# An attention and FFN block: last unit reordered, last products tile by tile, third chunk's turns moved

## The chip, the cores and the metric

The kernel runs on one core of one Trainium2 chip. The time is device microseconds of one execution of the program, from its first instruction to its last; the number compared is the median over executions.

## The reference

The input is x, 2 batches of 1024 tokens of 256 numbers. All is float32.

```python
mod = (_silu(L0_c) @ L0_wmod).reshape(L0_c.shape[0], 6, 1, -1)
sa, ca, ga, sb, cb, gb = ...                          # shifts, gains, gates per batch
h = _layernorm(x) * (1 + ca) + sa
x = x + ga * attention(h)                             # 16 heads of 128, rotary, causal, biases, @ Wo + bo
h = _layernorm(x) * (1 + cb) + sb
x = x + gb * (silu(h @ Wg.T) * (h @ Wu.T)) @ Wd.T     # hidden 704, int weights less 128, times row scales
```

## The kernel before

Each float32 operand of a matmul is held as two numbers of the fp32r format, a high part and a low part (value less high part). ScalarE makes the high part with a copy, and VectorE (DVE) or GpSimd (POOL) subtracts to make the low part. A product is then three matmuls (`three`, lines 1357 to 1362), or two in the FFN (`two`, lines 1364 to 1370), where the weights need no low part.

**Attention.** The work is 32 units: 8 pairs of heads, in each the two batches, in each the two heads. A unit has eight query tiles, taken in the order 0, 7, 1, 6, 2, 5, 3, 4 (`ORDER`, line 65), the steps. At a step, TensorE (PE) makes the scores of a tile into PSUM, DVE takes the row maxima (`row_max`), ScalarE the exponentials (`exponentials`), PE turns the probabilities in groups of up to four 128x128 blocks (`turn`), ScalarE copies the group (high) and DVE subtracts (low). The turned groups use two PSUM banks in turn, so a group waits for the subtraction two groups back. Between these stand pieces (`make`): projections, the products with the values (P0, P1), the products with Wo (W00, W01, W10, W11), and in the last two units the transposes of the FFN weights (L0 to L5 for gate and up, D0 to D2 for down). Pieces use the two banks of `ps_r` in turn; `wait_bank` (line 1372) makes a piece wait until the piece two before it has been read. For a W piece that is the sum on DVE (`wo_add`, line 1203); for a D piece it is ScalarE's copy (`down_out`).

What each engine does, and in which order, is written out in strings: `TENSOR_PLAN`, `SCALAR_PLAN`, `VECTOR_PLAN`, `POOL_PLAN`, with own versions for the last units (`PLANS_31` at line 123 is unit 31, the last, and `ENDING` at line 135 what comes behind it). A token such as `sum:W10-` is the sum of piece W10 of the unit before; `+` is the unit after. `unit_plan` (line 148) reads them. In the last unit the W pieces are those of unit 30.

**Between attention and FFN.** DVE takes the moments of each token's row (`x2_moments`) and the inverse roots (`x2_roots`, token `newton`). GpSimd multiplies the attention sums of four tiles by their gate (`gate_rows`), and adds them to x (`add_rows`). `gate_rows(2)` waits for all the sums of unit 30 (`y_added`), `gate_rows(3)` for the first roots. GpSimd also casts the down weights (`down_high`). ScalarE whitens the rows (`normal`), PE turns them (`turn_xn2`, 8 groups, two to a chunk), ScalarE applies gain and shift (`h2_out`), and GpSimd makes the low halves (`h2_low`).

**FFN.** Four chunks of 512 tokens, six hidden tiles each (the last of 64 rows), numbered n = 0 to 23. For each n: PE makes gate and up (`gate_up`, 8 matmuls, 4 for the last tile of a chunk), ScalarE the silu, DVE the product gu, ScalarE its high part (`gu_high`), GpSimd its low part, called the split (lines 755 to 770), counted by `gu_split`. There are eight slots for these, so from n = 8 on `gu_high` waits for the down products that read the slot (line 972). The down products of a chunk (`down`) stand behind tiles 2 and 3 of the next one, and DVE finishes them (`finish`: times gate, plus x). The last chunk's down products come at the end (lines 1698 to 1706): hidden tile by hidden tile, in each the four token tiles, in four PSUM banks; then DVE finishes the four tiles one by one, each stored by its own DMA.
Four tables place the extra work in that loop: `TURN_AT[n]` gives the groups that PE turns behind gate_up(n), and that ScalarE takes behind gu_high(n - 1) in its turn n; `LOW_AT[n]` the low halves that GpSimd makes ahead of split n; `NORMAL_AT` and `EARLY_NORMAL_AT` the whitening. `gate_up` waits for a chunk's two low halves at its first tile (line 1652).
Each engine's queue is in order: an instruction that waits holds all behind it.

Of the kernel before, what the change touches and what calls it, by code (L numbers as in the profile page):

```python
# [7 lines left out]
F32 = mybir.dt.float32  # L8
# [3 lines left out]
ALU = mybir.AluOpType  # L12
# [3 lines left out]
P = 128  # L16
# [9 lines left out]
NCH = TOK // CH  # L26
HM = (HID + P - 1) // P
HLAST = HID - (HM - 1) * P
# [24 lines left out]
GU = 8  # L53
# [2 lines left out]

NORMAL_AT = {6: 2}
EARLY_NORMAL_AT = {9: 3}
TURN_AT = {7: (4,), 8: (5,), 13: (6,), 14: (7,)}
LOW_AT = {0: (2,), 1: (3,), 8: (4, 5), 14: (6,), 15: (7,)}  # L60
PAUSE_AT = {1: 1}

OUT_TILES = [(2 * n, 2) for n in range(NTT // 2 - 2)] + [(n, 1) for n in range(NTT - 4, NTT)]
# [26 lines left out]
VECTOR_PLAN = """max:0 turn:6.0- turn:7.0- turn:7.1- max:1 low:P0- add:K0+ max:2 turn:0.0 add:Q0+ low:P1- max:3  # L90
# [32 lines left out]
PLANS_31 = {  # L123
    TENSOR_PLAN: """make:K0+ make:Q0+ scores:0 turn:6.0- turn:7.0- scores:1 scores:2 turn:7.1- make:P0- turn:0.0
        make:P1- scores:3 turn:1.0 make:W00- make:X scores:4 turn:1.1 turn:2.0 make:W01- scores:5 make:D0 turn:3.0
        make:W10- turn:3.1 turn:4.0 make:W11- scores:6 make:D1 turn:5.0 scores:7 make:D2 turn:5.1""",
    SCALAR_PLAN: """out:K0+ exp:7- turn:6.0- exp:0 out:Q0+ turn:7.0- turn:7.1- high:P0- turn:0.0 exp:1 exp:2
        high:P1- turn:1.0 turn:1.1 exp:3 turn:2.0 exp:4 gated:0 out:D0 turn:3.0
        exp:5 turn:3.1 turn:4.0 out:D1 exp:6 turn:5.0 out:D2 turn:5.1""",
    VECTOR_PLAN: """largest:3 max:0 turn:6.0- turn:7.0- turn:7.1- max:1 low:P0- max:2 turn:0.0 moments:0  # L130
        low:P1- max:3 sum:W00- turn:1.0 width:X max:4 turn:1.1 turn:2.0 sum:W01- max:5 turn:3.0 sum:W10- turn:3.1 turn:4.0
        sum:W11- max:6 max:7 turn:5.0 turn:5.1"""}


ENDING = {
# [2 lines left out]
    SCALAR_PLAN: """exp:7- turn:6.0- turn:7.0- turn:7.1- silu_table:0 high:P0- normal:0 normal:1 normal:2 normal:3  # L138
        normal:4 normal:5 normal:6 normal:7 high:P1- h2out:0 h2out:1 h2out:2 silu:0 h2out:3 silu:1 gu:0 silu:2 gu:1 silu:3 gu:2
        silu:4 gu:3 silu:5 gu:4""",  # L140
    VECTOR_PLAN: """turn:6.0- turn:7.0- turn:7.1- moments:1 newton:0 low:P0- low:P1- sum:W00- sum:W01-
        sum:W10- sum:W11- moments:2 ffn:0 ffn:1 moments:3 ffn:2 newton:2 ffn:3 ffn:4 ffn:5"""}
UNIT_29 = {SCALAR_PLAN: """out:K0+ exp:7- turn:6.0- exp:0 out:Q0+ turn:7.0- turn:7.1- high:P0- turn:0.0 exp:1 float:0 exp:2
        high:P1- high:K0+ high:Q0+ turn:1.0 float:1 out:K1+ turn:1.1 exp:3 turn:2.0 exp:4 out:Q1+ float:2 turn:3.0
# [3 lines left out]
def unit_plan(plan, u):  # L148

    out = []
    last = {0: PLANS_0, ALL_UNITS - 3: UNIT_29, ALL_UNITS - 2: PLANS_30, ALL_UNITS - 1: PLANS_31, ALL_UNITS: ENDING}
    plan = last.get(u, {}).get(plan, plan)
    for token in plan.split():
        what, name = token.rstrip("+-").split(":")  # L160
        v = u + {"+": 1, "-": -1}.get(token[-1], 0)
        if what == "split":
            which = "QKVO".index(name)
            n = v // UNITS + (which != WO)
            if v % UNITS == (0 if which == WO else 2) and n < PAIRS and v < ALL_UNITS:
                out.append((what, which, n))
        elif name[0] in "LDXB":
            kind = {"L": "late", "D": "down", "X": "width", "B": "bias"}[name[0]]
            out.append((what, v, (kind, int(name[1:] or 0))))
        elif what in ("float", "largest", "moments", "newton", "normal", "ffn", "silu", "gu", "xn", "xout", "xlow",  # L170
                      "gates", "bias", "gated", "xn2", "h2out", "silu_table", "mods"):
            out.append((what, v, (int(name),)))
        elif name[0] in "KQ":
            if 1 <= v < ALL_UNITS:
                out.append((what, v, ("qk", v, int(name[0] == "K"), int(name[1]))))
            elif v == ALL_UNITS and what in ("make", "out") and name[1] == "0":
                out.append((what, v, ("gate", "KQ".index(name[0]))))
        elif name[0] == "V":
            piece = ("v", 2 * (v // UNITS) + 1 + v % UNITS // 2, v % 2 * 2 + int(name[1]))
            if v >= 0 and piece[1] < 2 * PAIRS:  # L180
                out.append((what, v, piece))
        elif v == -1 and name[0] == "P":
            out.append((what, v, ("v", 0, 2 + int(name[1]))))
        elif 0 <= v < ALL_UNITS:
            if name[0] == "P":
                out.append((what, v, ("pv", v, int(name[1]))))
            elif name[0] == "W":
                out.append((what, v, ("wo", v, int(name[1]), int(name[2]))))
            else:
                out.append((what, v, tuple(int(x) for x in name.split("."))))  # L190
    return out
# [60 lines left out]
def build(nc, x, wq, bq, wk, bk, wv, bv, wo, bo, wq_gate, s_gate, wq_up, s_up, wq_down, s_down, c, wmod,  # L252
          cos, sin, out):
    with ExitStack() as ctx:
# [63 lines left out]
        newton = small("newton", [P, NTT], F32)  # L318
# [46 lines left out]
        gu_hi = at("gu_hi", A_PT, [P, GU, CH], F32R)  # L365
        gu_lo = at("gu_lo", A_PT + 2 * KB * GU, [P, GU, CH], F32R)
        gated = at("gated", A_ROPE + 11 * KB, [P, DIM], F32)
# [92 lines left out]
        gu_hi_ready = sem("gu_hi_ready")  # L460
        gu_split = sem("gu_split")
        down_made = sem("down_made")
# [33 lines left out]
        def gu_at(n, size):  # L496
            return gu[n % GU_F32 // 2][0:size, n % 2, :]
# [130 lines left out]
        def _(pool):  # L628
# [102 lines left out]
            def down_high(n):  # L731
                pool.wait_ge(down_full, n + 1)
                pool.tensor_copy(wd_hi[:, 2 * n:2 * n + 2, :], wd_full[:, 2 * n:2 * n + 2, :]).then_inc(down_ready, 1)
# [8 lines left out]
            gate_wo_low()  # L742
            down_high(0)
            down_high(1)
            pool.wait_ge(y_added, 1 + 4 * (ALL_UNITS - 1))
            gate_rows(2)
            down_high(2)
            pool.wait_ge(rstd2_ready, 1)
            gate_rows(3)
            add_rows(2, 6)  # L750
# [4 lines left out]
            for n in range(NCH * HM):  # L755
                size = P if n % HM < FULL else HLAST
                for j in LOW_AT.get(n, ()):
                    h2_low(j)
                if n in PAUSE_AT:
                    pool.wait_ge(rstd2_ready, PAUSE_AT[n] + 1)  # L760
                pool.wait_ge(gu_hi_ready, n + 1)
                low = gu_lo[:, n % GU, :]
                if size == HLAST:

                    low = gu_hi[HLAST:P, n % GU, :]
                    pool.wait_ge(gu_split, n)
                pool.tensor_tensor(low, gu_at(n, size), gu_hi[0:size, n % GU, :].bitcast(F32), ALU.subtract)\
                    .then_inc(gu_split, 1)
                if size == HLAST:
                    pool.wait_ge(gu_split, n + 1)  # L770
# [267 lines left out]
        def _(dve):  # L1038
# [317 lines left out]
        def _(pe):  # L1356
# [323 lines left out]
            def chunks(wide_weights):  # L1680

                ending = Span(ALL_UNITS, ALL_UNITS + 1)
                for what, x, piece in ending.work(TENSOR_PLAN):
                    if what == "ffn":
                        gate_up(*piece, wide_weights)
                    else:
                        do(ending, what, x, piece)
                for n in range(HM, NCH * HM):
                    chunk, m = divmod(n, HM)
                    gate_up(n, wide_weights)  # L1690
                    for j in TURN_AT.get(n, ()):
                        turn_xn2(j)
                    if m in (2, 3):
                        if n == HM + 2:
                            pe.wait_ge(down_ready, DOWN_PAIRS)
                        down(chunk - 1, m - 2, wide_weights)

                pe.wait_ge(out_ready, NTT - 4)
                pe.wait_ge(h2_hi_ready, GROUPS4)
                outs = [ps[:, j, 0:DIM] for ps in (ps_r, ps_t) for j in range(2)]  # L1700
                for m in range(HM):
                    pe.wait_ge(gu_split, (NCH - 1) * HM + m + 1)
                    for t in range(4):
                        ins = down_part(outs[t], t, NCH - 1, m, wide_weights)
                        if m == HM - 1:
                            ins.then_inc(down_made, 1)


            pe.wait_ge(wide_ready, 1)
# [36 lines left out]
```

## Time and profile before

| | us |
|---|---|
| median of 3 runs | 1036.28 (1036.2 to 1036.66) |
| the profiled execution, its own time | 1035.97 |
| its span in the trace | 1034.2 |
| PE busy | 1006.3 (97%) |
| DVE busy | 771.6 (75%) |
| ScalarE busy | 678.5 (66%) |
| GpSimd busy | 620.3 (60%) |

The time holds a little around the span. Busy shares are means over stages with different limits. In the rows, PE is the matmuls of TensorE and ACT is ScalarE; the idle time in square brackets stands in front of the instruction that ended it, with what released it. Times of a row are start and duration; matmuls are pipelined, so they start closer together than they last.

### The profile page before, as it was taken

What the parts mean: (1) busy time and instruction counts of PE and PEld (TensorE: products, weight loads), DVE (VectorE), ACT (ScalarE), POOL (GpSimd) and SP (SyncE); (2) the same over time, 40 slices, a digit from 0 to 9 for tenths busy, and PEclk for the clock granted to TensorE, in tenths of its full rate; (3) what the DMA queues carried; (4) which work ended last, traced back from release to release, by engine and by line L of the source; (5) the groups of instructions that cost most, each with busy time, mean ns of one, the idle gap of its engine ahead of it and who ended that gap; (6) DMA issues with size and microseconds to landing.
All of it is one profiled execution on the core that took longest, in us unless ns stands there. A gap on an engine that the chain in (4) does not pass through costs nothing.

```text
span 1034.2 us, 20453 instructions
## 1 busy us (share of the span) xinstructions
PE 1006.3 (97%) x6318; PEld 903.9 (87%) x6318; DVE 771.6 (75%) x1664; ACT 678.5 (66%) x1447; POOL 620.3 (60%) x472
## 2 busy tenths in 40 slices
PE   6989999999999999999999999999999999997997
PEld 5878999899989999999988999999999999986786
DVE  6668887777777877877777777777787777887644
ACT  5766766666666666666667666666666667767763
POOL 3365665666565755576555765665656655675654
PEclk9999999999999999999999999999999999999999
DMA  8412111211112211211112111221122113221011
GB/s 253 120 41 70 44 32 42 72 44 38 37 35 71 51 41 32 67 44 41 41 43 60 41 41 42 71 51 31 32 70 51 41 37 91 62 62 42 1 42 43
DMA packets 41987, 56.03 MB, mean 54 GB/s; under 512 B 5508, under 2 KB 25028, under 8 KB 41924
## 3 DMA queue, kind: packets, MB, share of 16 engines
q1 hardware_dynamic: 41924, 55.37, 20.8%
q8 instruction: 18, 0.29, 0.1%
q14 instruction: 45, 0.37, 0.1%
HBM read 19.69 MB, written 2.10 MB: 21 GB/s over the span
## 4 chain that ended last, share of the span: by engine, by line
PE 91%; DVE 2%; issue 2%; ACT 2%; POOL 1%; DMA 1%; SPq 0%; DVEq 0%; ACTq 0%; POOLq 0%
PE ps_r L1362 18%; PE ps_r L1361 18%; PE ps_r L1360 17%; PE ps_t L1519 12%; PE ps_s L1362 7%; PE ps_s L1361 7%; PE ps_s L1360 6%; PE ps_s L1367 2%; PE ps_s L1370 1%; PE ps_r L1369 1%; PE ps_r L1367 1%; PE ps_r L1458 1%; DMA wmod_a<-in_L_wmod 1%; POOL y L695 0%; ACT probs L907 0%
## 5 line engine op out<-in xcount | busy, mean ns | idle before, releaser
L651 POOL TENSOR_TENSOR swapped<-swapped,sin_sb 128x512 f32<-128x512 f32 x124 | 166.1, 1340 | 236.1 <-DMA swapped<-straight 235.6
L896 ACT ACTIVATE pT_hi<-ps_t 128x512 fp32r<-128x512 f32 (+3 forms) x384 | 186.8, 491 | 85.2 <-PE ps_t L1519 83.1
L1198 DVE TENSOR_TENSOR pT_lo<-ps_t,pT_hi 128x512 fp32r<-128x512 f32 (+3 forms) x384 | 202.3, 550 | 53.7 <-ACT pT_hi L896 53.6
L1263 DVE CUSTOM_DVE_ANT_0 ps_s<-ps_s,mask_wide 128x128 f32<-128x128 f32 (+7 forms) x256 | 194.5, 760 | 55.8 <-PE ps_s L1362 41.6
L661 POOL TENSOR_TENSOR qk_lo<-straight,qk_hi 128x512 fp32r<-128x512 f32 x124 | 162.2, 1322 | 112.3 <-ACT qk_hi L802 112.3
L907 ACT ACTIVATE probs<-ps_s,neg_max 128x128 f32<-128x128 f32 (+7 forms) x256 | 190.3, 743 | 44.1 <-DVE neg_max L1263 37.0
L1519 PE MATMUL ps_t<-ident,probs 128*128 128x128 f32 x1152 | 185.6, 274 | 6.5 <-DVE pT_lo L1198 5.9
L652 POOL TENSOR_TENSOR straight<-straight,cos_sb 128x512 f32<-128x512 f32 x124 | 180.9, 1459 | 0.0
L1126 DVE TENSOR_TENSOR straight<-straight,swapped 128x512 f32<-128x512 f32 x126 | 129.1, 1025 | 32.5 <-POOL straight L652 32.0
L1519 PEld LDWEIGHTS ps_t<-ident,probs 128*128 128x128 f32 x1152 | 134.3, 140 | 11.3 <-issue 4.9
L1360 PE MATMUL ps_s<-qk_hi 128*128 128x512 f32 (+3 forms) x384 | 139.9, 364 | 0.1
L1360 PE MATMUL ps_r<-pT_hi,v_hi 128*128 128x512 f32 (+3 forms) x384 | 134.2, 349 | 0.0
L1362 PE MATMUL ps_s<-qk_hi,qk_lo 128*128 128x512 f32 (+3 forms) x384 | 133.0, 346 | 0.0
L1362 PE MATMUL ps_r<-pT_hi,v_lo 128*128 128x512 f32 (+3 forms) x384 | 132.6, 345 | 0.0
L1361 PE MATMUL ps_s<-qk_lo,qk_hi 128*128 128x512 f32 (+3 forms) x384 | 132.4, 345 | 0.0
L1361 PE MATMUL ps_r<-pT_lo,v_hi 128*128 128x512 f32 (+3 forms) x384 | 132.1, 344 | 0.0
L1222 DVE SCALAR_TENSOR_TENSOR y<-ps_r,inv_sum,y 128x256 f32<-128x256 f32 x248 | 108.4, 479 | 26.6 <-PE ps_r L1362 22.1
L1360 PE MATMUL ps_r<-hT_hi,w_hi 128*128 128x512 f32 x256 | 106.6, 416 | 0.3 <-DVE v_lo L1132 0.3
L1362 PE MATMUL ps_r<-hT_hi,w_lo 128*128 128x512 f32 x256 | 100.9, 394 | 0.0
L1361 PE MATMUL ps_r<-hT_lo,w_hi 128*128 128x512 f32 x256 | 100.8, 394 | 0.0
L813 ACT ACTIVATE o_hi<-ps_r 128x512 fp32r<-128x512 f32 x64 | 38.4, 599 | 90.4 <-PE ps_r L1362 90.3
L789 ACT ACTIVATE straight<-ps_r,cols 128x512 f32<-128x512 f32 x63 | 43.4, 689 | 62.3 <-PE ps_r L1362 57.4
(195 smaller groups left out, 2221.1 us busy)
## 6 DMA issues: line engine op xcount, KB each, us to landing
swapped<-straight SPq DMA_DIRECT2D x252, 128.0 KB, 2.3
x_in<-in_L_attn_x SPq DMA_DIRECT2D x4, 512.0 KB, 5.5
w_raw<-in_L_attn_Wk SPq DMA_DIRECT2D x8, 256.0 KB, 3.3
w_raw<-in_L_attn_Wq SPq DMA_DIRECT2D x8, 256.0 KB, 3.5
w_raw<-in_L_attn_Wv SPq DMA_DIRECT2D x8, 256.0 KB, 3.6
wo_all<-in_L_attn_Wo SPq DMA_DIRECT2D x1, 2048.0 KB, 9.9
wo_raw<-in_L_attn_Wo SPq DMA_DIRECT2D x8, 256.0 KB, 2.7
x<-in_L_attn_x SPq DMA_DIRECT2D x4, 512.0 KB, 4.1
```

Source lines behind the costliest of these rows:

```text
L651: pool.tensor_tensor(swapped[:, q, :], swapped[:, q, :], sin_sb[:, cs], ALU.mult)
L652: pool.tensor_tensor(straight[:, q, :], straight[:, q, :], cos_sb[:, cs], ALU.mult).then_inc(rotated, 1)
L661: pool.tensor_tensor(lo, rope_buffers(piece)[0][:, RANK[piece] % 2, :], hi.bitcast(F32), ALU.subtract)\
L896: nc.scalar.activation(turned_at(ORDER[step], k0, k1)(pT_hi), ps_t[:, (T_FIRST[step] + j) % 2, 0:(k1 - k0) * P].rearrange("p (k q) -> p k ...
L907: nc.scalar.activation(probs[:, P_AT[step] * P:(P_AT[step] + t + 1) * P], ps_s[:, step % 2, 0:(t + 1) * P], ACT.Exp, bias=neg_max[:, t:t + ...
L1126: nc.vector.tensor_tensor(here[:, q, :], here[:, q, :], there[:, q, :], ALU.add).then_inc(qk_sum, 1)
L1198: nc.vector.tensor_tensor(turned_at(t, k0, k1)(pT_lo), ps_t[:, (T_FIRST[step] + j) % 2, 0:(k1 - k0) * P].rearrange("p (k q) -> p k q", q=P ...
L1263: nc.vector.tensor_tensor_reduce(rows, rows, mask_wide[:, SEQ - n_keys:SEQ], -1.0, -MASKED, ALU.add, ALU.min, accum_out=neg_max[:, t:t + 1 ...
L1360: nc.tensor.matmul(out, shi, mhi, start=first, stop=False)
L1361: nc.tensor.matmul(out, shi, mlo, start=False, stop=False)
L1362: return nc.tensor.matmul(out, slo, mhi, start=False, stop=last)
L1519: ins = nc.tensor.transpose(ps_t[:, bank, at_ * P:at_ * P + P], probs[:, (P_AT[step] + k) * P:(P_AT[step] + k) * P + P], ident[:, :])
```

## The change

In the last unit, the three pieces D0 to D2 stand ahead of W10 and W11, on all engines; on DVE the sum of W01 moves behind the maximum of step 5, W10's to the end of the unit, and W11's to behind the last subtraction of the unit, into `ENDING` (token `sum:W11--`, for which `unit_plan` counts the signs). GpSimd casts the third pair of down weights ahead of `gate_rows(2)`.
In the FFN, chunk 2's two groups (4 and 5) are turned one hidden tile later, and their low halves made at n = 9 and 10.
In the end, the last products are made token tile by token tile: tiles 0, 1, 2 over hidden tiles 0 to 3, then the rest of each, then all of tile 3. The last split (n = 23) is done by DVE instead of GpSimd.

```diff
-TURN_AT = {7: (4,), 8: (5,), 13: (6,), 14: (7,)}
-LOW_AT = {0: (2,), 1: (3,), 8: (4, 5), 14: (6,), 15: (7,)}
+TURN_AT = {8: (4,), 9: (5,), 13: (6,), 14: (7,)}
+LOW_AT = {0: (2,), 1: (3,), 9: (4,), 10: (5,), 14: (6,), 15: (7,)}

 PLANS_31 = {
     TENSOR_PLAN: """make:K0+ make:Q0+ scores:0 turn:6.0- turn:7.0- scores:1 scores:2 turn:7.1- make:P0- turn:0.0
         make:P1- scores:3 turn:1.0 make:W00- make:X scores:4 turn:1.1 turn:2.0 make:W01- scores:5 make:D0 turn:3.0
-        make:W10- turn:3.1 turn:4.0 make:W11- scores:6 make:D1 turn:5.0 scores:7 make:D2 turn:5.1""",
+        make:D1 turn:3.1 scores:6 make:D2 turn:4.0 make:W10- scores:7 turn:5.0 make:W11- turn:5.1""",
     SCALAR_PLAN: """out:K0+ exp:7- turn:6.0- exp:0 out:Q0+ turn:7.0- turn:7.1- high:P0- turn:0.0 exp:1 exp:2
-        high:P1- turn:1.0 turn:1.1 exp:3 turn:2.0 exp:4 gated:0 out:D0 turn:3.0
-        exp:5 turn:3.1 turn:4.0 out:D1 exp:6 turn:5.0 out:D2 turn:5.1""",
+        high:P1- turn:1.0 turn:1.1 exp:3 turn:2.0 exp:4 gated:0 turn:3.0 out:D0
+        exp:5 turn:3.1 out:D1 turn:4.0 out:D2 exp:6 turn:5.0 turn:5.1""",
     VECTOR_PLAN: """largest:3 max:0 turn:6.0- turn:7.0- turn:7.1- max:1 low:P0- max:2 turn:0.0 moments:0
-        low:P1- max:3 sum:W00- turn:1.0 width:X max:4 turn:1.1 turn:2.0 sum:W01- max:5 turn:3.0 sum:W10- turn:3.1 turn:4.0
-        sum:W11- max:6 max:7 turn:5.0 turn:5.1"""}
+        low:P1- max:3 turn:1.0 sum:W00- width:X max:4 turn:1.1 turn:2.0 max:5 sum:W01- turn:3.0 turn:3.1
+        max:6 turn:4.0 max:7 turn:5.0 sum:W10- turn:5.1"""}

 ENDING = {
-    VECTOR_PLAN: """turn:6.0- turn:7.0- turn:7.1- moments:1 newton:0 low:P0- low:P1- sum:W00- sum:W01-
+    VECTOR_PLAN: """turn:6.0- turn:7.0- turn:7.1- sum:W11-- moments:1 newton:0 low:P0- low:P1- sum:W00- sum:W01-

-        v = u + {"+": 1, "-": -1}.get(token[-1], 0)
+        v = u + token.count("+") - token.count("-")

             down_high(1)
+            down_high(2)
             pool.wait_ge(y_added, 1 + 4 * (ALL_UNITS - 1))
             gate_rows(2)
-            down_high(2)
             pool.wait_ge(rstd2_ready, 1)

                 pool.wait_ge(gu_hi_ready, n + 1)
                 low = gu_lo[:, n % GU, :]
+                if n == NCH * HM - 1:
+                    break
                 if size == HLAST:

+            last = NCH * HM - 1
+            dve.wait_ge(gu_hi_ready, last + 1)
+            dve.wait_ge(gu_split, last)
+            nc.vector.tensor_tensor(gu_hi[HLAST:P, last % GU, :], gu_at(last, HLAST),
+                                    gu_hi[0:HLAST, last % GU, :].bitcast(F32), ALU.subtract).then_inc(gu_split, 1)
             for j in range(4):
                 dve.wait_ge(down_made, (NCH - 1) * 2 + j + 1)
                 finish(NTT - 4 + j, 1, (ps_r, ps_t)[j // 2][:, j % 2, None, 0:DIM])

-                for m in range(HM):
-                    pe.wait_ge(gu_split, (NCH - 1) * HM + m + 1)
-                    for t in range(4):
+                for t, parts in ((0, range(0, 4)), (1, range(0, 4)), (2, range(0, 4)), (0, range(4, HM)),
+                                 (1, range(4, HM)), (2, range(4, HM)), (3, range(0, HM))):
+                    for m in parts:
+                        pe.wait_ge(gu_split, (NCH - 1) * HM + m + 1)
                         ins = down_part(outs[t], t, NCH - 1, m, wide_weights)
-                        if m == HM - 1:
-                            ins.then_inc(down_made, 1)
+                    if HM - 1 in parts:
+                        ins.then_inc(down_made, 1)
```

## Rows read from the trace of the kernel before

**Rows 1.** The page's chain that ended last: share of the span by engine.
```profile
PE 91%; DVE 2%; issue 2%; ACT 2%; POOL 1%; DMA 1%; SPq 0%; DVEq 0%; ACTq 0%; POOLq 0%
```
**Rows 2.** Windows: stretch, length, busy PE, PEld, DVE, ACT, POOL, granted clock, DMA, GB/s.
```profile
33.90:37.20 3.30, 3.30 (x12) 2.65 (x11) 2.63 (x6) 2.69 (x6) 0.00 (x0) 0.51 0.72 235
930.00:950.00 20.00, 16.88 (x115) 14.79 (x115) 17.32 (x50) 13.13 (x28) 8.83 (x13) 1.00 0.16 54
1030.00:1031.00 1.00, 0.00 (x0) 0.00 (x0) 0.97 (x3) 0.00 (x0) 0.00 (x0) 0.71 0.39 131
```
**Rows 3.** Timeline of PE in the last unit: start, duration, instruction, idle before and releaser.
```profile
933.49 0.41 PE L1519 MATMUL ps_t<-ident,probs 128*128 128x128 f32 x2 [0.77 <-DVE pT_lo L1198]
935.55 0.60 PE L1454 MATMUL ps_r<-ident,f_down 128*128 128x128 f32 x4
936.34 0.36 PE L1360 MATMUL ps_r<-wo_hi,o_hi 128*128 128x256 f32 x1
...
943.65 1.26 PE L1519 MATMUL ps_t<-ident,probs 128*128 128x128 f32 x8 [1.05 <-DVE pT_lo L1198]
```
**Rows 4.** Timeline of DVE, last unit to the moments, and the first finish.
```profile
928.18 1.04 DVE L1241 TENSOR_SCALAR var<-mv 128x4 f32<-128x4 f32 x1
...
935.10 0.87 DVE L1222 SCALAR_TENSOR_TENSOR y<-ps_r,inv_sum,y 128x256 f32<-128x256 f32 x2
935.88 0.96 DVE L1263 CUSTOM_DVE_ANT_0 ps_s<-ps_s,mask_wide 128x768 f32<-128x768 f32 x1
...
944.95 1.72 DVE L1198 TENSOR_TENSOR pT_lo<-ps_t,pT_hi 128x512 fp32r<-128x512 f32 x3 [1.06 <-ACT pT_hi L896]
946.58 1.40 DVE L1235 BATCH_NORM_STATS2 bn<-x 128x6 f32<-128x256 f32 x4
...
948.43 0.17 DVE L1241 TENSOR_SCALAR var<-mv 128x4 f32<-128x4 f32 x1
...
1027.74 0.43 DVE L1338 TENSOR_TENSOR ps_r<-ps_r,gb_row 128x256 f32<-128x256 f32 x1 [3.44 <-PE ps_r L1645]
```
**Rows 5.** Timeline of POOL (GpSimd) up to the FFN.
```profile
926.80 2.39 POOL L702 TENSOR_TENSOR x<-x,y 128x1024 f32<-128x1024 f32 x1
...
951.10 2.38 POOL L695 TENSOR_TENSOR y<-y,ga_row 128x1024 f32<-128x1024 f32 x1 [6.39 <-DVE shift_x L1254]
...
958.10 2.52 POOL L738 TENSOR_TENSOR hT_lo<-h_32a,hT_hi 128x512 fp32r<-128x512 f32 x2
```
**Rows 6.** Timeline of PE in the FFN: chunk starts, the turn, the last products.
```profile
960.68 0.50 PE L1367 MATMUL ps_s<-hT_hi,wg_hi 128*128 128x512 f32 x1 [0.51 <-POOL hT_lo L738]
...
977.20 0.63 PE L1593 MATMUL ps_t<-ident,xn 128*128 128x128 f32 x4 [0.78 <-ACT xn L941]
...
990.05 0.47 PE L1367 MATMUL ps_s<-hT_hi,wg_hi 128*128 128x512 f32 x1
...
1007.18 0.50 PE L1367 MATMUL ps_s<-hT_hi,wg_hi 128*128 128x512 f32 x1 [0.65 <-POOL hT_lo L738]
...
1027.42 0.40 PE L1645 MATMUL ps_r<-wd_hi,gu_hi 128*128 128x256 f32 x2
```
**Rows 7.** Timeline of ACT (ScalarE): the exponential of step 3.
```profile
933.25 1.00 ACT L907 ACTIVATE probs<-ps_s,neg_max 128x896 f32<-128x896 f32 x1
```
**Rows 8.** Timeline of POOL in the FFN: low halves (hT_lo) and splits (gu_lo).
```profile
981.92 2.56 POOL L738 TENSOR_TENSOR hT_lo<-h_32c,hT_hi 128x512 fp32r<-128x512 f32 x2
988.03 2.73 POOL L767 TENSOR_TENSOR gu_lo<-gu_a,gu_hi 128x512 fp32r<-128x512 f32 x2 [3.55 <-ACT gu_hi L973]
...
1004.59 1.30 POOL L767 TENSOR_TENSOR gu_lo<-gu_b,gu_hi 128x512 fp32r<-128x512 f32 x1 [4.99 <-ACT gu_hi L973]
...
1020.85 2.74 POOL L767 TENSOR_TENSOR gu_lo<-gu_a,gu_hi 128x512 fp32r<-128x512 f32 x2 [6.20 <-ACT gu_hi L973]
1024.11 1.29 POOL L767 TENSOR_TENSOR gu_lo<-gu_b,gu_hi 128x512 fp32r<-128x512 f32 x1 [0.52 <-ACT gu_hi L973]
```
**Rows 9.** The line of a DVE subtraction with both operands in SBUF: min/median/max ns.
```profile
L1107 DVE TENSOR_TENSOR hT_lo<-h,hT_hi x8: 675/691/1243, 14.6 to 46.3; 128x512 fp32r<-128x512 f32 x8
```

## The prediction

> **What bounds the kernel now.** The chain of waits comes first: PE holds 91% of it [rows 1]. The reader is to see that the only things that move the end are PE's products and the few places where PE, or the short chains that stand in for it, wait. All of this change lies behind 930 us, so the slices come next: in 930 to 950 PE is busy 16.88 of 20 us and DVE 17.32, so DVE is as full as PE there [rows 2]. The timelines then show who waits for whom. In the last unit PE waits 0.77 us at 933.49, and 1.05 us at 943.65, for DVE's subtractions, and DVE waits 1.06 us at 944.95 for ScalarE [rows 3, 4]. Behind it stands a chain without PE: the last subtraction, then moments (from 946.58) and roots on DVE, then GpSimd's row gate, two row adds and two low halves back to back from 951.10 to 960.6, behind which the first gate product starts at 960.68 [rows 4, 5, 6]. In the FFN, PE waits 0.78 us ahead of the turn at 977.20, and starts chunk 2 at 990.05 and chunk 3 at 1007.18 [rows 6]. The tail is four DVE finishes, one after the other, from 1027.74 [rows 4].
>
> **Part A, the last unit.** I walk the new order with the rows' spacings (start to start): four transposes 0.43 us, turn of 4, 3, 2 blocks 0.35, 0.25, 0.15; W piece 0.80; scores 5, 6, 7: 1.11, 0.70, 1.05; on DVE a 128x512 subtraction 0.60, W sum 0.79 (0.99 with its reciprocal), maxima of step 5, 6, 7: 0.87, 0.60, 0.75. The subtraction of turn 1.0 now precedes the sum of W00, so the 0.77 us wait at 933.49 goes. What is late next: W01 needs W00's sum (933.35), so it starts at 933.5, ends at 934.3, and scores 5 needs the exponential that starts at 933.25 and takes 1.0 us with its read-out [rows 7]: 934.45, against 934.44 before. So nothing is gained up to there.
>
> Then a new wait. D0 runs at 935.55 as before, but the next piece, D1, uses the PSUM bank of W01, whose sum now stands behind the maximum of step 5. That maximum starts when scores 5 is done (935.85), 0.87 us, the sum 0.79 and its tail, release 0.15 (as in row 933.49 behind the subtraction): D1 starts at 937.7. Before, W10 used that bank at 936.34, since the sum (935.10) went ahead of the maximum (935.88) [rows 3, 4]. PE stands 1.4 us; behind it are turn 3.1, scores 6 and all else. From 937.74 the order D1, turn 3.1, scores 6, D2, turn 4.0, W10, scores 7, turn 5.0, W11, turn 5.1 takes 0.43 + 0.25 + 0.70 + 0.43 + 0.25 + 0.80 + 1.05 + 0.35 + 0.80 + 0.15 = 5.2 us: 943.0. DVE does the step 7 maximum at 942.0, subtraction 5.0 to 943.6, the sum of W10 to 944.55, subtraction 5.1 to 944.9; turn 7.0 needs that one's bank and goes at 945.1 (before: in the pair at 943.65). Its copy 0.6 and subtraction 0.6 behind its 0.6 of turn, then 7.1: DVE is free at 947.19 instead of 946.58, **0.61 later**. The idle 1.06 us of DVE is spent, and the new waits cost more.
>
> Next on DVE is now the sum of W11, **0.79**, ahead of the moments (start 947.98). And GpSimd's gate of rows 8 to 11, 2.36 us long, which waits for this sum, no longer runs at 941.8 but at 948.1 to 950.5, beside the moments. The variance instruction there took 0.17 us with GpSimd idle (948.43), and 1.04 us (928.18 to 929.22) when a GpSimd add ran from 926.80 to 929.19: it ended with it [rows 4, 5]. The new one is due at 949.83 (1.85 behind the moments' start, as before) and would end at 950.54 instead of 950.00: **0.54**. All of A: 0.61 + 0.79 + 0.54 = **+1.94** on the release of the roots, which GpSimd's gate of rows 12 to 15 shows (951.10 to 953.04). The chain on GpSimd follows back to back and gives nothing back, and whitening on ScalarE, the W pieces and their sums hang on the same release, so the first gate product goes from 960.68 to 962.6. Moving the third cast of down weights ahead of the gate costs nothing: it stands in GpSimd's idle, and D2 is earlier.
> The Trainium skill (GPSIMD Engine Reference, Key points) says that GpSimd shares its SBUF interfaces with VectorE, with contention for instructions in a 2-port mode or with two SBUF inputs. The rows agree for the variance; how long the wait is, the page doesn't give. Without that rule A would be 1.40.
> Bounds of A: below, DVE's whole 1.06 us idle goes and only the sum is added, -0.3; above, both orders' stalls add (1.4 of D1, 0.79, 0.54): +2.7. I take 1.94, the walk.
>
> **Part B, chunk 2's turns.** Gained: PE no longer waits for the whitened rows; the next gate_up, 8 products of 0.23 us, goes first. The wait at 977.20 is 0.78 us of idle and 0.15 in which the last product only drains (0.39 long at a spacing of 0.23): 0.93 [rows 6]. Each turn costs PE 0.35 us wherever it stands. So the end of down(0,1), and all that it releases, comes 0.93 earlier.
> Lost: on GpSimd, low 4 and 5 ran at 981.92 to 984.48, ahead of the split of product 8. That split waits for gu_hi 8, and gu_hi 8 for down(0,1), whose slot it writes: S = 988.03 [rows 8]. Now low 4 is queued behind split 8, and low 5 behind split 9. ScalarE's h2_out(5) stands behind gu_hi 8 too (TURN_AT 9), then silu 10 and gu_hi 9; by ScalarE's 0.5 to 0.7 us for each of these, gu_hi 9 is there at S + 2.4, when GpSimd has done split 8 and low 4 (S + 2.5): in time. Gate_up(12) needs low 5. Before it started at 990.05 = S + 2.02. Chunk 3 has a small copy of the new order: one split and one low behind its down (S = 1004.59), and PE starts at 1007.18, S + 2.59 [rows 6, 8]. One more pair is 2 x 1.25: S + 5.09. The loss is 3.07, and B = 3.07 - 0.93 = **+2.14**. Nothing later absorbs it: PE's later waits hang on its own down pieces. PE, which stood 0.24 us there, will stand 3.3 us, the longest wait of the FFN.
> Bounds of B: -0.93 if the low halves stay hidden; above, +2.14 and the clock (below).
>
> **Part C, the last products.** Before: 44 products of 0.12, the last at about 1027.8, DVE's first finish at 1027.74 (tile 0's last product at 1027.42, + 0.32), four at a spacing of 0.80 [rows 4, 6]. New order, in old times from 1022.62: tile 0's m = 3 needs split 21, which ends at 1023.59 (second of the pair at 1020.85): it could go at 1023.34, so 0.36 is lost; the 24 products of the first three groups end at 1025.86; m = 4 needs split 22, done at 1025.40 [rows 8]. The last split on DVE starts when 22 is done, 1025.48, and takes 0.69 as a like subtraction of SBUF operands [rows 9]: 1026.17, PE at 1026.32, finish at +0.32: 1026.64. Tile 3 is ready at 1028.7, before DVE's fourth finish at 1029.04, so DVE's four still set the end: **-1.10**. Bounds: 0, if the split takes 1.8 us; -1.5 without both waits.
>
> **Sum.** 1.94 + 2.14 - 1.10 = +2.98 us. On the profiled execution, 1035.97 (span 1034.2), that is 1038.95; the median 1036.28 is 0.31 above it, so 1039.26. I forecast **1039.3**. What a measurement can tell from no change is 0.2%, 2.07 us.
>
> **Rivals** (each from 1036.28).
> *The clock falls.* In the 3.3 us wait ahead of gate_up(12) PE may lose its clock. For: at the end PE's last product is at 1027.9 and the slice 1030 to 1031 has 0.71, so it fell 2.4 us behind it [rows 2]; there it goes from 2.4 to 1.2 GHz. Against: no wait in the kernel's middle shows it, and none is that long. Price: it was low once while PE worked, behind a run of small products, for at least the 3.3 us from 33.9 to 37.2, with a granted clock near 0.5 [rows 2]. Half of such a stretch is lost, 1.5 to 1.6: 1040.8.
> The Trainium skill (TensorE: Matmul & The Clock Gate, HAM oscillation) warns that waits can leave the next products at the lower clock; by it this rival would be the likelier. No row shows a wait this long inside the products, so I keep it second.
> *The last unit costs nothing.* If the waits of D1 and of turn 7.0 fall into time that PE and DVE stood anyway, A is 0: +1.03, 1037.3. For: PE stood 3.1 us in four waits between 932 and 946 (two of them are in rows 3), so there is time to fall into. Against: each of these hung on DVE's order, and D1's place in it is new.
> *Faster.* GpSimd's low halves of chunk 2 are done inside the 3.5 us in which it idles between 984.5 and 988.0, so B is -0.93; A gives back DVE's 1.06 less the sum, -0.3; C -1.10: -2.3, 1034.0. It decides at one point: gate_up(12) starts no later than S + 2.02. Against: GpSimd takes its instructions in order, and a split that can't start before S now stands before each low half.
> *It does not reach what it says.* B's low halves hidden and A as walked: -0.1, 1036.2.
>
> **Chances.** Forecast 0.55, clock 0.15, last unit free 0.16, faster 0.10, no change 0.04. Slower by over 0.2% holds the first two but a little of the first: 0.68; faster 0.11; within 0.21. The range, 1036.4 to 1041.6, leaves out the faster case and the no-change case, and holds A's and B's upper bounds in part.
>
> **What would show it.** A: D1 at 937.7 with a wait of 1.4 us on DVE; the sum of W11 behind the last subtraction; a long variance instruction beside GpSimd's gate; that gate at 953. B: no wait ahead of the turn, and one of about 3.3 us on GpSimd's hT_lo ahead of chunk 2, with GpSimd's order split, low, split, low. C: first finish 1.1 us earlier than by the shift, four in a row. It is wrong if chunk 2 starts before S + 2.5, or GpSimd's gate of rows 12 to 15 before 951.5.

## The result and the profile after

| | median us | runs | ratio to before, 95% interval |
|---|---|---|---|
| before | 1036.2 (1035.77 to 1037.36) | 7 | |
| changed | 1040.29 (1038.76 to 1042.78) | 7 | 1.0041 (1.0029 to 1.0052) |

The change costs 4.1 us, which is more than the 0.2% that can be told from no change. The forecast was 1039.3 with a range to 1041.6. The profiled execution of the changed kernel took 1040.92 (span 1039.1, 4.9 more than before). One execution of the last kernel in the table of experiments took 1241.65 us at a mean granted clock of 0.753, and its ratio leaves it out.

To see where 4.9 us lie, I put the same landmark events of both traces side by side and compare the distances between them. The landmarks are D0 (the first transposes of down weights), GpSimd's gate of rows 12 to 15, the first products of chunks 0, 2 and 3, the last down products and the first finish.

| from, to | before | after | difference | forecast |
|---|---|---|---|---|
| span start, D0 | 935.55 | 935.76 | +0.21 | 0 |
| D0, gate of rows 12 to 15 (part A) | 15.55 | 17.52 | +1.97 | +1.94 |
| gate, gate_up(0) | 9.58 | 9.55 | -0.03 | 0 |
| gate_up(0), gate_up(12) (part B) | 29.37 | 31.41 | +2.04 | +2.14 |
| gate_up(12), gate_up(18) | 17.13 | 18.76 | +1.63 | 0 (rival: 1.5 to 1.6) |
| gate_up(18), first finish (part C) | 20.56 | 19.46 | -1.10 | -1.10 |
| first finish, span end | 6.46 | 6.64 | +0.18 | 0 |

Part A first. The timeline of PE of the changed kernel, in the last unit (start, duration, instruction, idle before it and releaser) answers to [rows 3]:

```profile
933.61 0.38 PE L1367 MATMUL ps_r<-wo_hi,o_hi 128*128 128x256 f32 x1 [0.46 <-DVE y L1224]
...
935.76 0.60 PE L1461 MATMUL ps_r<-ident,f_down 128*128 128x128 f32 x4
...
937.88 0.66 PE L1461 MATMUL ps_r<-ident,f_down 128*128 128x128 f32 x4 [1.08 <-DVE y L1224]
...
943.99 0.63 PE L1526 MATMUL ps_t<-ident,probs 128*128 128x128 f32 x4 [0.57 <-DVE pT_lo L1200]
945.31 1.04 PE L1526 MATMUL ps_t<-ident,probs 128*128 128x128 f32 x5 [0.70 <-DVE pT_lo L1200]
```

The 0.77 us wait of before is gone; W01 waits 0.46 us for the sum of W00, and D0 comes no earlier, as the forecast had it. New is the wait of D1 for the sum of W01 on DVE: D1 starts 2.12 us behind D0, where the forecast had 2.15. The row has 1.08 us of idle for it; counted from the end of the turn before, by its spacing of 0.35, it is 1.33, for which the forecast had 1.4. DVE's own timeline shows why, and what follows at the end of the unit ([rows 4] of before):

```profile
936.07 0.97 DVE L1265 CUSTOM_DVE_ANT_0 ps_s<-ps_s,mask_wide 128x768 f32<-128x768 f32 x1 [0.68 <-PE ps_s L1369]
...
936.95 0.87 DVE L1224 SCALAR_TENSOR_TENSOR y<-ps_r,inv_sum,y 128x256 f32<-128x256 f32 x2
...
946.61 0.89 DVE L1200 TENSOR_TENSOR pT_lo<-ps_t,pT_hi 128x512 fp32r<-128x512 f32 x2 [0.63 <-ACT pT_hi L898]
947.41 0.87 DVE L1224 SCALAR_TENSOR_TENSOR y<-ps_r,inv_sum,y 128x256 f32<-128x256 f32 x2
948.20 1.40 DVE L1237 BATCH_NORM_STATS2 bn<-x 128x6 f32<-128x256 f32 x4
...
950.04 0.75 DVE L1243 TENSOR_SCALAR var<-mv 128x4 f32<-128x4 f32 x1
...
1031.30 0.69 DVE L1355 TENSOR_TENSOR gu_hi<-gu_b,gu_hi 64x512 fp32r<-64x512 f32 x1 [1.20 <-POOL gu_lo L769]
1032.46 0.43 DVE L1340 TENSOR_TENSOR ps_r<-ps_r,gb_row 128x256 f32<-128x256 f32 x1 [0.48 <-PE ps_r L1652]
```

The reader is to see the sum of W11 at 947.41, between the last subtraction and the moments, and the variance instruction of 0.75 us at 950.04, for which [rows 4] have 0.17. The timeline of GpSimd (POOL) has its cause: gate_rows(2) runs from 948.36 to 950.76, and the variance instruction ends at 950.79.

```profile
948.36 2.40 POOL L695 TENSOR_TENSOR y<-y,ga_row 128x1024 f32<-128x1024 f32 x1 [6.35 <-DVE y L1224]
953.28 2.35 POOL L695 TENSOR_TENSOR y<-y,ga_row 128x1024 f32<-128x1024 f32 x1 [2.52 <-DVE shift_x L1256]
...
989.20 1.30 POOL L769 TENSOR_TENSOR gu_lo<-gu_a,gu_hi 128x512 fp32r<-128x512 f32 x1 [6.22 <-ACT gu_hi L975]
990.45 1.29 POOL L738 TENSOR_TENSOR hT_lo<-h_32c,hT_hi 128x512 fp32r<-128x512 f32 x1
991.69 1.27 POOL L769 TENSOR_TENSOR gu_lo<-gu_a,gu_hi 128x512 fp32r<-128x512 f32 x1
992.91 1.27 POOL L738 TENSOR_TENSOR hT_lo<-h_32c,hT_hi 128x512 fp32r<-128x512 f32 x1
```

The last four of these rows are part B: split 8, low 4, split 9, low 5, back to back ([rows 8] have the two lows at 981.92, ahead of split 8). GpSimd idles 6.22 us ahead of split 8, and then holds up chunk 2. PE in the FFN, against [rows 6]:

```profile
962.83 0.50 PE L1374 MATMUL ps_s<-hT_hi,wg_hi 128*128 128x512 f32 x1 [0.49 <-POOL hT_lo L738]
...
980.27 0.60 PE L1600 MATMUL ps_t<-ident,xn 128*128 128x128 f32 x4
...
994.24 0.61 PE L1374 MATMUL ps_s<-hT_hi,wg_hi 128*128 128x512 f32 x1 [3.09 <-POOL hT_lo L738]
994.64 0.63 PE L1377 MATMUL ps_s<-hT_lo,wg_hi 128*128 128x512 f32 x1
...
998.46 0.40 PE L1377 MATMUL ps_s<-hT_lo,wg_hi 128*128 128x512 f32 x1
998.69 0.39 PE L1374 MATMUL ps_s<-hT_hi,wg_hi 128*128 128x512 f32 x1
...
1013.00 0.50 PE L1374 MATMUL ps_s<-hT_hi,wg_hi 128*128 128x512 f32 x1 [0.66 <-POOL hT_lo L738]
```

The turn at 980.27 has no wait any more. Gate_up(12) starts at 994.24, 5.04 us behind split 8 (S = 989.20), and PE stood 3.09 us for GpSimd's low half. The first products behind this wait start 0.43 us apart, and from 998.2 on 0.23. The windows of the changed kernel (stretch, length, busy PE, PEld, DVE, ACT, POOL, granted clock, DMA, GB/s) give the granted clock:

```profile
991.20:994.20 3.00, 0.00 (x0) 0.00 (x0) 1.38 (x2) 1.44 (x3) 3.00 (x4) 1.00 0.17 57
990.00:995.00 5.00, 1.91 (x8) 1.24 (x7) 1.50 (x2) 2.64 (x5) 5.00 (x5) 0.95 0.15 52
995.00:998.00 3.00, 3.00 (x9) 2.34 (x8) 0.08 (x1) 1.20 (x2) 0.97 (x2) 0.52 0.00 0
998.00:1001.00 3.00, 3.00 (x17) 2.47 (x16) 1.43 (x2) 1.96 (x4) 1.49 (x2) 1.00 0.00 0
```

The granted clock was 1.00 through the whole wait. In slices of 0.1 us it goes to its lower level of 1.2 GHz at 994.5, 0.24 us behind the first product of chunk 2, and is back at 2.4 GHz at 997.9. So PE paid for it in the 3.4 us in which it worked again. That is the rival "the clock falls". The page's chain answers to [rows 1]: DVE and GpSimd have one per cent more each, and the two new waits lead through them.

```profile
PE 92%; DVE 3%; POOL 2%; issue 1%; ACT 1%; DMA 1%; SPq 0%; DVEq 0%; ACTq 0%; POOLq 0%
```

### The profile page after: what moved, and what is told of

It is laid out like the page before. It is cut to its first block, busy times and chain, and to the rows that moved or that the text cites. A ratio compares the mean times of both kernels' runs of the same rounds, so it can differ in the third digit from the quotient of the medians.

```text
span 1039.1 us, 20453 instructions
## 1 busy us (share of the span) xinstructions
PE 1009.6 (97%) x6318; PEld 906.2 (87%) x6318; DVE 772.0 (74%) x1665; ACT 678.4 (65%) x1447; POOL 619.2 (60%) x471
## 4 chain that ended last, share of the span: by engine, by line
PE 92%; DVE 3%; POOL 2%; issue 1%; ACT 1%; DMA 1%; SPq 0%; DVEq 0%; ACTq 0%; POOLq 0%
PE ps_r L1369 18%; PE ps_r L1368 18%; PE ps_r L1367 17%; PE ps_t L1526 12%; PE ps_s L1369 7%; PE ps_s L1368 7%; PE ps_s L1367 7%; PE ps_s L1374 2%; PE ps_s L1377 1%; PE ps_r L1374 1%; PE ps_r L1376 1%; PE ps_s L1542 1%; PE ps_r L1465 1%; POOL hT_lo L738 1%; DVE ps_s L1265 1%
```

## The experiments

Theory: three separate prices, A +1.97 (two thirds of it from the sum of W11 and from GpSimd's gate, which waits for that sum), B +2.04 (low halves queued behind splits) and the clock +1.63 behind B's wait, less C's 1.10. The rivals are that the parts hide or lengthen each other, that the clock is not a price of this change, and, for A, that the new PSUM wait is most of it.

The time of an execution moves by a microsecond and more for reasons outside the change. D0 starts anywhere from 934.57 to 936.67 in the fourteen traces, and from the first finish to the span's end takes 6.3 to 7.2 us. So beside each median stands the path in the profiled execution from D0 to the first finish, 92.19 us before. "Over before" is the ratio less 1, times 1036. Two kernels ran once only, for their traces, and have no ratio.

| kernel | median us | runs | ratio, 95% interval | over before | D0 to first finish |
|---|---|---|---|---|---|
| changed | 1040.29 | 7 | 1.0041 (1.0029 to 1.0052) | +4.2 | +4.51 |
| A alone | 1038.54 | 11 | 1.0024 (1.0015 to 1.0033) | +2.5 | +1.99 |
| B alone | 1039.39 | 5 | 1.0035 (1.0022 to 1.0049) | +3.6 | +3.62 |
| C alone | 1035.32 | 11 | 0.9993 (0.9984 to 1.0002) | -0.7 | -1.10 |
| A and C | 1037.54 | 11 | 1.0014 (1.0005 to 1.0023) | +1.5 | +0.85 |
| changed, lows at 8 and 9 | 1037.70 | 11 | 1.0015 (1.0006 to 1.0024) | +1.6 | +0.57 |
| changed, one filler | 1040.04 | 6 | 1.0034 (1.0022 to 1.0046) | +3.5 | +3.81 |
| changed, both fillers | 1039.49 | 5 | 1.0036 (1.0022 to 1.0049) | +3.7 | +2.94 |
| A, sum of W11 early | 1036.68 | 11 | 1.0008 (0.9999 to 1.0017) | +0.8 | +0.61 |
| A, sum of W01 early | 1039.39 | 1 | | | +1.58 |
| changed, two-input variance | 1040.52 | 1 | | | +4.49 |
| before, both turns at 8 | 1035.26 | 11 | 0.9990 (0.9981 to 0.9999) | -1.0 | -0.98 |
| the same and C | 1034.16 | 11 | 0.9983 (0.9974 to 0.9992) | -1.8 | -2.06 |

The traces' column lies inside each interval, or just off its edge (lows at 8 and 9, 0.57 where the interval begins at 0.6). The interval of C alone holds 1, so its gain is shown by the path and not by the median.

### Each part alone

A alone is the edits of the plans of unit 31 and `ENDING` with `down_high(2)`; B alone the two tables; C alone the last split on DVE and the new order of the last products.

> Part A alone (unit 31's order, the sum of W11 behind the last subtraction, the third cast ahead of the gate), the FFN as before. The walk: +1.9 us (1.0019). Rival, that the last unit costs nothing and the whole loss is chunk 2's: within 0.3 of zero. Rival, that the parts feed each other: far from 1.9.

> Part B alone (the tables TURN_AT and LOW_AT). Queue theory: +2.1 us where PE keeps its clock and +3.7 where it loses it for about 3.4 us behind the 3.3 us wait ahead of gate_up(12); granted clock 0.997 in the first kind of run and 0.995 in the second, so a wider spread than before's, most runs of the second kind. Rival, that the low halves stay hidden: -0.9.

> Part C alone (last products tile by tile, last split on DVE). The walk: -1.1 us. Rival, that the split on DVE or PE's waits eat it: 0.

> The change without B: A and C. If the parts add, +1.9 - 1.1 = +0.8 us, with a granted clock of 0.997 and a spread like before's, since no wait of 3 us is left. If the lost clock came from A's 2.3 us wait ahead of the turns of whitened rows, it would show here too: clock 0.995 and about +2.4.

All four came out near the theory. On the path the three parts add up to what all of them give together: 1.99 + 3.62 - 1.10 = 4.51. A alone has the D1 wait of 1.08 and 17.53 us from D0 to the gate. C alone takes 19.46 us from gate_up(18) to the first finish. B alone shows both its own price and the clock's:

```profile
991.08 0.50 PE L1367 MATMUL ps_s<-hT_hi,wg_hi 128*128 128x512 f32 x1 [3.10 <-POOL hT_lo L738]
...
1009.84 0.50 PE L1367 MATMUL ps_s<-hT_hi,wg_hi 128*128 128x512 f32 x1 [0.65 <-POOL hT_lo L738]
```

That is 18.76 us from chunk 2 to chunk 3 where it was 17.13.

A and C together brought what only the rival of that text had named: a fall of the clock at A's own wait. PE waits 2.26 us ahead of the transposes at 955.08, and the clock falls at 955.5, 0.4 us behind their start. Windows of that kernel:

```profile
956.00:959.00 3.00, 2.73 (x13) 2.44 (x12) 1.55 (x4) 3.00 (x6) 3.00 (x2) 0.51 0.00 0
959.00:962.00 3.00, 2.74 (x23) 2.54 (x23) 2.48 (x8) 1.14 (x3) 3.00 (x3) 1.00 0.00 0
```

There it cost nothing, where the rival had 1.6: GpSimd's adds and low halves, 9.55 us from the gate to gate_up(0), were the path, and PE had time to lose beside them.

### The low halves one place earlier

```diff
-LOW_AT = {0: (2,), 1: (3,), 9: (4,), 10: (5,), 14: (6,), 15: (7,)}
+LOW_AT = {0: (2,), 1: (3,), 8: (4,), 9: (5,), 14: (6,), 15: (7,)}
```

> The whole change with GpSimd's two low halves one tile earlier: LOW_AT has 8: (4,), 9: (5,) instead of 9: (4,), 10: (5,). Queue theory: GpSimd does low 4 in its idle, then split 8 from S, low 5 at S + 1.25, done at S + 2.5; then gate_up(12) waits for DVE's product 10 instead, which hangs on silu 10 behind h2_out(5): S + 2.75 instead of S + 5.04. 2.3 us less, and no fall of the clock: 1.6 more. Against the change -3.9, against before about +0.2. Rival, that ScalarE's order (h2_out(5) behind gu_hi 8) is what costs: hardly any gain.

Only the path came out as expected. Gate_up(12) starts 2.77 us behind split 8 instead of 5.04, and the clock stays at 1.00:

```profile
992.16 0.47 PE L1374 MATMUL ps_s<-hT_hi,wg_hi 128*128 128x512 f32 x1 [0.83 <-DVE gu_b L1301]
```

From D0 to the first finish it is 3.94 us less than in the changed kernel (4.51 - 0.57), where 3.9 was expected; the median fell 2.6, and stands 1.2 above the expectation. Its trace has the clock down behind A's wait as well (0.50 in 956 to 959), at no cost in this one execution. Its three slowest executions (1038.40 to 1038.60) have the lowest mean clock, 0.993, so lost clock may be part of the 1.2; how much is not shown.

### Fillers in the waits

Products that nobody reads keep PE busy while it waits; the waits themselves stay. `pe.wait_ge` only makes sure that `ps_t` has been read.

```diff
+                    if n == 2 * HM:
+                        pe.wait_ge(h2_hi_ready, 5)
+                        for _ in range(14):
+                            nc.tensor.matmul(ps_t[:, 0, :], mask_wide[:, 0:P], mask_wide[:, 0:CH], start=True, stop=True)
```

> The whole change, with 14 products of 128x512 bf16 (their result is never read) put ahead of gate_up(12), where PE waits 3.1 us for GpSimd. They take 3.0 us of that wait. If the clock falls because PE stands there, it stays at 2.4 GHz through chunk 2's first tiles, gate_up(12) to gate_up(18) takes 17.1 us as before instead of 18.8, and the time falls by 1.6 against the change: about +2.6 against before. If the lower clock had another cause, +4.1 as now.

The first half of this held, the time did not. The windows of this kernel:

```profile
953.00:957.00 4.00, 1.74 (x16) 1.63 (x15) 1.10 (x4) 3.39 (x7) 3.35 (x2) 0.98 0.00 0
957.00:963.00 6.00, 5.18 (x25) 4.89 (x24) 3.49 (x9) 3.80 (x7) 6.00 (x4) 0.50 0.00 0
990.00:1002.00 12.00, 11.93 (x58) 8.30 (x56) 4.15 (x7) 8.36 (x15) 8.82 (x7) 1.00 0.07 23
```

Ahead of gate_up(12) the clock stayed up, and chunk 2 took 17.19 us instead of 18.76. But in this execution it fell behind A's wait, 1.0 us behind the start of the transposes, stayed down for 6.8 us, twice as long as in A and C, and this time PE's W pieces were late: 10.47 us from the gate to gate_up(0) instead of 9.55. Of the 1.57 regained, 0.92 were lost there. So I filled that wait too, with 9 such products ahead of `turn_xn2(0)`:

> The changed kernel with products that nobody reads in both long waits of PE: 9 of 128x512 (0.23 us each, 2.1 us) ahead of the transposes behind the last unit, where the kernel with one filler waited 2.26 us and then ran at a granted clock of 0.50 from 957 to 963, and 14 (3.2 us) ahead of gate_up(12), as there. Theory (the clock's price is real and moves from one wait to the other): the granted clock is 0.97 or more in 953 to 967 and in 990 to 1002; from GpSimd's gate of rows 12 to 15 to gate_up(18) takes 58.1 to 58.2 us (59.72 in the changed kernel, 59.01 with one filler: 59.72 less 1.6), and the median is 1039.2, 2.9 above the kernel before (the sum 1.94 + 2.04 - 1.09 of waits alone). Rival (the clock costs the changed kernel's median little, since most of its executions keep it): the spans in the trace are as said, but the median stays at 1040.0, where one filler had it.

```profile
953.00:957.00 4.00, 3.59 (x23) 2.19 (x20) 0.42 (x1) 4.00 (x9) 4.00 (x2) 1.00 0.00 0
957.00:963.00 6.00, 4.32 (x28) 3.65 (x29) 5.37 (x15) 4.49 (x7) 5.40 (x4) 1.00 0.00 0
990.00:1002.00 12.00, 11.93 (x64) 8.58 (x63) 3.75 (x5) 8.36 (x15) 8.72 (x8) 1.00 0.07 23
```

The clock is at full speed in both places, and from the gate to gate_up(18) takes 58.14 us (expected 58.1 to 58.2). On the path the theory holds: +2.94 is the sum of the waits alone. The median is 0.3 above the expected 1039.2, though the kernel before was 0.5 lower beside it (1035.83 for 1036.29): by the ratio it is 3.7 over before, 0.5 less than the changed kernel where 1.6 was expected. The two intervals overlap from 3.0 to 5.1, so the medians settle neither the theory nor the rival. The changed kernel itself goes from 1038.76 at a mean clock of 0.997 to 1042.78 at 0.990, so what the clock costs differs from execution to execution, and 1.63 is its price in the traces alone.

### What part A is made of

A alone, with the sum of W01 ahead of the maximum again, so that D1 has no wait:

```diff
-        ... turn:2.0 max:5 sum:W01- turn:3.0 turn:3.1
+        ... turn:2.0 sum:W01- max:5 turn:3.0 turn:3.1
```

> Part A alone, but on DVE the sum of W01 again ahead of the maximum of step 5. D1's wait of 1.08 us must go (D1 right behind turn 3.0). If that wait is what makes A's walk late, GpSimd's second row gate comes about 1 us earlier, 16.5 us behind D0's start (part A alone: 17.53; before: 15.55). If ScalarE's queue (exponential 5, two copies of D, two of turns, back to back) is next in line, only 0.3 earlier: 17.2.

D1 follows at once, and ScalarE's copy of a D piece is late instead, for which W10 waits at 940.63. Timeline of PE of this kernel:

```profile
936.67 0.60 PE L1454 MATMUL ps_r<-ident,f_down 128*128 128x128 f32 x4
937.54 0.60 PE L1454 MATMUL ps_r<-ident,f_down 128*128 128x128 f32 x4
...
940.63 0.39 PE L1360 MATMUL ps_r<-wo_hi,o_hi 128*128 128x256 f32 x1 [0.70 <-ACT wd_full L935]
```

From D0 to the gate is 17.19, so the 1.1 us wait was worth 0.34 of A's 1.98. Then the other half, the sum of W11 in an idle gap of DVE between two subtractions:

```diff
-    VECTOR_PLAN: """turn:6.0- turn:7.0- turn:7.1- sum:W11-- moments:1 ...
+    VECTOR_PLAN: """turn:6.0- sum:W11-- turn:7.0- turn:7.1- moments:1 ...
```

> Part A alone, with the sum of W11 put between the subtractions of turn 6.0 and turn 7.0, where DVE has an idle gap, instead of behind the last one. Theory (the sum on DVE's path and GpSimd's gate of rows 8 to 11, which waits for that sum and holds DVE's variance instruction, are 0.79 and 0.54 of part A): the gate starts 1.2 us earlier and is over when the variance instruction comes, which takes 0.17 again instead of 0.75; D0 to GpSimd's gate of rows 12 to 15 takes 16.3 us (17.53 with part A, 15.55 before), and the median is 1037.0 to 1037.3 (1038.5 with part A). Rival (most of part A is the new PSUM wait of D1 and the later subtractions, which this edit leaves): 17.2 or more, median 1038.2.

```profile
945.38 0.87 DVE L1222 SCALAR_TENSOR_TENSOR y<-ps_r,inv_sum,y 128x256 f32<-128x256 f32 x2
946.17 0.88 DVE L1198 TENSOR_TENSOR pT_lo<-ps_t,pT_hi 128x512 fp32r<-128x512 f32 x2
946.96 1.40 DVE L1235 BATCH_NORM_STATS2 bn<-x 128x6 f32<-128x256 f32 x4
948.39 0.38 DVE L1238 BATCH_NORM_AGGREGATE mv<-bn 128x2 f32<-128x6 f32 x4
948.81 0.17 DVE L1241 TENSOR_SCALAR var<-mv 128x4 f32<-128x4 f32 x1
```

GpSimd's gate now runs from 946.33 to 948.73, the variance instruction comes at 948.81 and is 0.17 again, and D0 to the gate takes 16.21 us (expected 16.3). One token moved gives 1.32 of the 1.98, just what the forecast had for these two terms (0.79 + 0.54). Part A is still not a gain.

Last, whether the variance instruction waits because of its form:

```diff
-nc.vector.tensor_scalar(var[:, part], mv[:, part, 1], EPS, None, ALU.add)
+nc.vector.scalar_tensor_tensor(var[:, part], mv[:, part, 1], EPS, mv[:, part, 1], ALU.add, ALU.max)
```

> The changed kernel with the variance instruction of 128x4 as one that reads two tensors from SBUF (the smaller term is added and a maximum taken with the same input, which changes no value that matters) instead of one tensor and a constant. It runs beside GpSimd's gate of rows 8 to 11. Theory (DVE's instruction waits until GpSimd's is over whatever its number of inputs): it ends within 0.1 us of GpSimd's gate, 0.75 us long as in the changed kernel, and GpSimd's gate of rows 12 to 15 starts 17.5 us behind D0. Rival (only the form with one input and a constant waits): it takes 0.17 to 0.25 us, and the 17.5 become 17.0.

```profile
947.38 1.40 DVE L1237 BATCH_NORM_STATS2 bn<-x 128x6 f32<-128x256 f32 x4
948.81 0.38 DVE L1240 BATCH_NORM_AGGREGATE mv<-bn 128x2 f32<-128x6 f32 x4
949.22 0.74 DVE L1243 SCALAR_TENSOR_TENSOR var<-mv 128x4 f32<-128x4 f32 x1
```

The same 0.74, ending with GpSimd's gate (947.54 to 949.95). The moments beside the same gate are not held: 1.40 us, and 0.38 for their aggregates, and 1.40 is what [rows 4] have with GpSimd idle. The Trainium skill (SBUF — State Buffer, SBUF: two separate sides) says that the pair of ports shared by VectorE and GpSimd is an exclusive lock, taken for the whole instruction by whichever starts first, and asked for by DVE in a 2-port mode or with two SBUF inputs. The end times agree with that (949.96 for DVE's instruction, 949.95 for GpSimd's); which of the forms uses which mode no run here shows.

### A better version

Before, with both turns of chunk 2 behind tile 8, where the rows are whitened in time and the low halves still stand ahead of split 8:

```diff
-TURN_AT = {7: (4,), 8: (5,), 13: (6,), 14: (7,)}
+TURN_AT = {8: (4, 5), 13: (6,), 14: (7,)}
```

> Before, with both turns of chunk 2 behind gate_up(8) (TURN_AT has 8: (4, 5) instead of 7: (4,), 8: (5,)) and the low halves where they were. The wait at 977.20 goes, the low halves stay in GpSimd's idle: -0.9 us. Rival, that moving the turns costs by itself: +1 or more.

> The kernel before with two edits only: both turns of chunk 2 (4 and 5) behind tile 8, which measured 1.0 less, and the last products tile by tile (part C), which took 1.10 out of the trace and 0.7 off the median. The two lie in different stretches, so they add: gate_up(0) to gate_up(12) 28.4 us (29.37 before), gate_up(18) to the first finish 19.5 (20.56 before), median 1034.4 to 1034.6, some 1.8 below the kernel before. Rival (part C's gain is eaten when what stands ahead comes earlier, the splits of products 21 and 22 being then late): 1035.2.

The second of these kernels has part C as well. In its timeline of GpSimd the low halves stand at 980.37, ahead of split 8:

```profile
980.37 2.53 POOL L738 TENSOR_TENSOR hT_lo<-h_32c,hT_hi 128x512 fp32r<-128x512 f32 x2
986.64 1.29 POOL L769 TENSOR_TENSOR gu_lo<-gu_a,gu_hi 128x512 fp32r<-128x512 f32 x1 [3.74 <-ACT gu_hi L975]
```

The two gains add: 28.42 us from gate_up(0) to gate_up(12), 19.46 from gate_up(18) to the first finish, -2.06 on the path, and a median of 1034.16. The ratio 0.9983 (0.9974 to 0.9992) is a small gain whose interval lies below 1. It is the fastest kernel of the study, though its interval overlaps those of its two parts.

## Why the prediction was right, and where it was not

**Part A, +1.94 forecast, +1.97 measured.** The walk held step by step. The forecast has D0 0.21 earlier than this trace; with that added its events stand at 947.40 for the end of the subtractions (the sum starts at 947.41), 948.19 for the moments (948.20), 950.75 for the end of the variance instruction (950.79). The wait of D1 came at its place, and the early-sum kernel confirmed 0.79 + 0.54 as one term of 1.32. What the forecast overrated is D1's wait as a cause: without it only 0.34 comes back, because ScalarE's copy of the D piece is next.

**Part B, +2.14 forecast, +2.04 measured.** The gain, 0.93, is 0.98 in the trace: split 8 stands 26.37 us behind gate_up(0) instead of 27.35. The loss followed from the order split, low, split, low and came at S + 5.04 for S + 5.09. The kernel with both turns at 8 shows that the gain could be had without the loss. The rival "faster" needed gate_up(12) at S + 2.02, and the lows did not stay hidden.

**Part C, -1.10 forecast, -1.10 measured.** DVE's last split took the 0.69 us of [rows 9], and the first finish came 4.03 us behind the first of the last products, where the walk had 4.02.

**The sum, and the clock.** Here the forecast failed in one step, "I keep it second". The trace shows the fall and its price of 1.63, within 0.1 of the 1.5 to 1.6 that the rival had from [rows 2]. The rival's time, 1040.8, is 0.5 above the measured 1040.29; the forecast's 1039.3 is 1.0 below. That the time still lies in the stated range is owed to the range, which held the rival too, and not to the sum, which lacks this term. The argument against was that no wait in the kernel's middle shows a fall and none is that long, and the second half of that sentence undid the first. All three traces with that wait unfilled have the fall, 0.24, 0.49 and 0.74 us behind the wait's end.

The row at the kernel's end, where the clock had fallen 2.4 us behind PE's last product, was the only one for a pause of this length, and it was a lucky one. In the other traces the fall at the end comes 2.0 to 5.2 us behind the last product, and only in five of the fourteen within 3.1 us. The kernel with C alone has 4.6 us without a product at the full clock:

```profile
1028.40:1033.00 4.60, 0.00 (x0) 0.00 (x0) 1.19 (x3) 0.00 (x0) 0.00 (x0) 1.00 0.30 97
```

So the ends show that a pause can cost the clock, but not when it falls. The Trainium skill (TensorE: Matmul & The Clock Gate, HAM oscillation) warns that the products behind a wait can start at the lower clock. The changed kernel agrees in what it costs (0.50 from 994.5 on); the page has the fall within the wait, and here it came behind the wait's end. That the medians of the two filled kernels did not drop by the full 1.6 stays open; their intervals are 2.5 and 2.8 us wide.

**"The last unit costs nothing"** is refuted by A alone: 1.99 on the path, +2.5 in the median, with an interval above 1. (Its own sum, 2.14 - 1.10, is 1.04 and not 1.03.) **"It does not reach what it says"** fell with B's low halves.

## What to carry to other kernels

An engine whose queue is in order doesn't hide work that is moved behind an instruction that waits: GpSimd idled 6.2 us ahead of split 8, and the low half behind that split still held up PE for 3.1. Before one moves a step later to remove a wait of 0.8, ask on each engine which instruction it now stands behind, and how long that one waits. Price a new wait of TensorE twice, once for its length and once for the half clock behind it (3.4 us at 1.2 GHz cost 1.63 here), and look for the fall behind the wait, not in it. One pause of like length that keeps its clock, or loses it, does not tell what the next execution does.

## What was not expected of the hardware

The clock also fell behind the waits of 2.2 to 2.3 us ahead of the transposes at 955, 0.1 to 1.0 us behind their end: in three of the seven traces that have this wait unfilled (A and C, one filler, lows at 8 and 9), and not in the others (the changed kernel, A alone, W01 first, the two-input form). It was low for 3.4 us in two of them and for 6.8 in the third. From the gate to gate_up(0) takes 9.55, 9.55 and 10.47 us in them, so it cost 0, 0 and 0.92. The waits of 0.7 us there show no fall (five traces), nor does the one of 1.29 in the early-sum kernel (one trace). Fourteen products of 128x512, 3.2 us, kept it up ahead of gate_up(12), in two traces of two. A fall needs no wait, either: in all fourteen traces the clock falls between 31.5 and 34.2 us and stays down for 3.4 us (nine traces) or 6.8 (five). In the trace of before this is at 33.8, and PE's rows show no idle time in the 4 us ahead, only, from 29.1 on, 32 products of 128x2 and a few larger ones.

A DVE instruction of 0.17 us on 128x4 values takes up to 0.75 (1.04 in [rows 4]) when a GpSimd instruction of 2.4 us is running, and ends within 0.03 us of it. Beside GpSimd's low half of 1.29 us at 963.47 of the changed kernel it takes 0.64, and ends at 964.78 for 964.76.
